# Output projection inside the attention loop, one-hot pairs and bias additions among the key-value products, and the second normalisation by groups of row tiles

## The reference, cut to what matters

```python
xn = layernorm(x)
x = x + gnn(xn) + mix(xn)          # first normalisation
x = x + ffn(layernorm(x))          # second normalisation

# mix: linear attention, 8 heads of 64
q, k, v = split(xn @ w_qkv)
q, k = elu(q) + 1, elu(k) + 1
kv = k.T @ v                        # for each head
z = 1 / (q @ sum(k) + 1e-6)
mix = concat((q @ kv) * z) @ w_out + b_out

# gnn: four experts of two mean-aggregating layers, two chosen for each row
gates = softmax(xn @ gate_W + gate_b); top2(gates)
# ffn: a shared expert and the best 3 of 16 experts, each silu(gate) * up, then down
```

## Time and profile before

| | us |
|---|---|
| median of three runs (1374.01 to 1377.84) | 1375.5 |
| profiled execution | 1378.77 |
| its span | 1376.5 |
| PE busy | 1276.0 (93%) |
| VectorE busy | 717.5 (52%) |
| ScalarE busy | 426.8 (31%) |
| GpSimd busy | 250.6 (18%) |

### The profile page before, as it was taken

How to read it: one execution, slowest core, us unless ns; L and a number is a source line. 1 busy time by engine, 2 the same in 40 slices (tenths; PEclk the granted TensorE clock), 3 DMA queues, 4 the chain that set the end, 5 groups by cost and what they waited for, 6 DMA issues and landing times.

```text
span 1376.5 us, 20320 instructions
## 1 busy us (share of the span) xinstructions
PE 1276.0 (93%) x6004; PEld 978.7 (71%) x6005; DVE 717.5 (52%) x1906; ACT 426.8 (31%) x760; POOL 250.6 (18%) x297
## 2 busy tenths in 40 slices
PE   5799999989999999999999988598999999999994
PEld 4454452668787887888788877377878888887883
DVE  5797765736454355236423624465454455446552
ACT  2022222335344134224322323321342233225331
POOL 2300000303302202310232013114701111111111
PEclk8599996899999999999999999799999999999998
DMA  9500000063524514441545153116673355237522
GB/s 352 217 1 1 1 31 0 1 196 120 154 70 146 142 58 146 101 137 50 161 104 134 54 160 81 74 16 188 186 227 61 56 143 138 55 54 211 149 50 34
DMA packets 72211, 146.62 MB, mean 107 GB/s; under 512 B 11826, under 2 KB 12560, under 8 KB 72148
## 3 DMA queue, kind: packets, MB, share of 16 engines
q1 hardware_dynamic: 54468, 99.41, 21.4%
q0 software_dynamic: 17680, 46.43, 16.0%
HBM read 87.15 MB, written 58.67 MB: 106 GB/s over the span
## 4 chain that ended last, share of the span: by engine, by line
PE 75%; DMA 7%; DVE 7%; issue 5%; POOL 3%; ACT 1%; DVEq 0%; SPq 0%; POOLq 0%; ACTq 0%
PE B L1869 19%; PE B L1721 15%; PE B L1513 15%; PE B L1728 8%; PE B L1664 7%; PE B L1805 3%; PE B L1556 2%; DMA xg<-slots 2%; PE B L1752 2%; DMA arow<-counts,idxA 2%; POOL chosen_ids L605 1%; POOL slots L720 1%; PE B L1850 1%; DMA out_rows<-y,y_tok 1%; PE B L1911 1%
## 5 line engine op out<-in xcount | busy, mean ns | idle before, releaser
L1869 PE MATMUL B<-GUWH,xtH 128*128 (+1 forms) x344 | 145.1, 422 | 0.8 <-DVE xtL L1346 0.8
L711 POOL DMA_INDIRECT out_rows<-y,y_tok x44 | 68.5, 1558 | 381.5 <-ACT y L944 371.5
L1869 PE MATMUL B<-GUWH,xtL 128*128 (+1 forms) x344 | 136.6, 397 | 0.0
L1869 PE MATMUL B<-GUWL,xtH 128*128 (+1 forms) x344 | 136.5, 397 | 0.0
L1090 DVE TENSOR_SCALAR key<-iota_key,keyT,neg_win 128x320 bf16<-128x320 int16 x240 | 89.7, 374 | 0.0
L1664 PE MATMUL B<-GH,conv 128*128 128x512 f32 x210 | 82.2, 392 | 3.0 <-ACT conv L836 3.0
L1664 PE MATMUL B<-GL,conv 128*128 128x512 f32 x210 | 81.9, 390 | 0.0
L1869 PE MATMUL B<-DNWH,htH 128*128 x176 | 75.3, 428 | 1.7 <-DVE htL L1346 1.7
L1869 PEld LDWEIGHTS B<-GUWH,xtL 128*128 128x128 f32 x344 | 65.0, 189 | 15.8
L830 ACT ACTIVATE hsXH<-XT 128x512 fp32r<-128x512 f32 x40 | 25.3, 631 | 162.9 <-PE B L1721 160.8
L1089 DVE TENSOR_SCALAR low<-iota_low,lowT 128x128 bf16<-128x128 int16 x240 | 62.9, 262 | 22.6 <-PE B L1556 21.4
(11 more groups left out here) (364 smaller groups left out, 2839.2 us busy)
## 6 DMA issues: line engine op xcount, KB each, us to landing
raw<-in_L_ffn_expert_gate_up SPq DMA_DIRECT2D x16, 1024.0 KB, 5.3
slots<-fill SPq DMA_DIRECT2D x5, 2112.0 KB, 19.9
hidden<-tr SPq DMA_DIRECT2D x40, 256.0 KB, 2.0
xg<-slots SPq DMA_DIRECT2D x34, 264.0 KB, 2.7
raw<-in_L_ffn_expert_down SPq DMA_DIRECT2D x8, 1024.0 KB, 5.8
counts<-astage SPq DMA_DIRECT2D x10, 648.0 KB, 3.0
W1R<-in_L_gnn_Wr SPq DMA_DIRECT2D x4, 1024.0 KB, 5.9
W1R<-in_L_gnn_Wl SPq DMA_DIRECT2D x4, 1024.0 KB, 8.3
```

What stands on the lines that cost most here:

```text
L711: pool.indirect_dma_start(out=out, out_offset=bass.IndirectOffsetOnAxis(ap=y_tok[:, 0:1], axis=0), in_=y[:, :], in_offset=None, compute_op ...
L1869: last = pe.matmul(bank, rows[a][:, k, :], weights[b](k), start=k == 0 and n == 0, stop=k == KD - 1 and n == 2)
```

## The change

- **Front.** The gate logits stand behind the query products 1 to 10, a tile each, in bank `B[5]`; the windows' bounds behind query product 0. VectorE's work on the gate is cut in four: `gate_maximum` behind the query features, `gate_softmax`, `gate_choice` and `expert_ranks` between the last residuals.
- **Features.** ScalarE computes Relu of -t and then Exp of minus that (`below`); VectorE's minimum is gone.
- **Window pairs.** Six among the query products, thirteen among the key-value products (three of them between a key and a value product), one behind the denominators, none among the output rows.
- **Bias and low parts.** VectorE adds `bo` a tile at a time in the key-value loop, and forms `XN_L` in the attention loop; ScalarE makes `XN_H` ahead of that loop. GpSimd does neither.
- **Denominators.** The three chunks go to rows 0, 32 and 64 of one bank (`DEN` = 72 rows), with one addition and one reciprocal; the masks `heads` have 72 rows, and GpSimd builds them behind the last key and value products.
- **Output projection.** Rows 0 to 5 stand in the attention loop, behind its steps 5, 6, 7, 9, 10 and 11 (`O_AFTER`), rows 6 to 9 behind it. The counts of the adjacency are ready (`at_ready`) ahead of the last residuals, and the aggregation starts with the sum of its first tile, its `count_rows` coming behind.
- **Second normalisation** (`normalise_groups`): statistics, square root and rows of one group of three tiles at a time; `variance(c+1)` comes ahead of `rows(c)`.
- **Last addition.** `add_chosen` reads the row index ahead of its wait for the epilogue.

```diff
-PAIR_AFTER_Q = {2 * p + 1: p for p in range(6)}
-PAIR_AFTER_KV = {i: 6 + i for i in range(NT)}
-PAIR_AFTER_O = {2 * q + 1: 16 + q for q in range(4)}
+PAIR_AFTER_Q = {2: 0, 4: 1, 6: 2, 8: 3, 10: 4, 11: 5}
+PAIR_AFTER_K = {2: 8, 5: 12, 8: 16}
+PAIR_AFTER_V = {0: 6, 1: 7, 2: 9, 3: 10, 4: 11, 5: 13, 6: 14, 7: 15, 8: 17, 9: 18}
+PAIR_AFTER_DEN = 19
+O_AFTER = {5: 0, 6: 1, 7: 2, 9: 3, 10: 4, 11: 5}
+DEN = 72
...
@@ gpsimd
-        pool.wait_ge(S["small_in"], 16 * 3)
-        pool.wait_ge(S["xn_done"], NT)
-        pool.tensor_tensor(X[:, :, :], X[:, :, :], bo[:, :].unsqueeze(1).to_broadcast([P, NT, D]), ALU.add)\
-            .then_inc(S["bias_added"], 1)
-
-        for i in range(NT):
-            pool.wait_ge(S["xn_h"], i + 1)
-            pool.tensor_tensor(XN_L[:, i, :], XN[:, i, :], XN_H[:, i, :].bitcast(F32), ALU.subtract).then_inc(S["xn_l"], 1)
+        pool.wait_ge(S["k_pe"], NT)
+        pool.wait_ge(S["v_pe"], NT)
+        link(pool.memset(heads[:, :, :, :], 1.0))
+
+        link(pool.affine_select(out=heads[:, :, :, :], in_=heads[:, :, :, :], compare_op=ALU.is_ge, fill=0.0,
+                                base=0, pattern=[[32 * P // 2, 3], [P, HP], [1, P]], channel_multiplier=-P // 2))
...
-            wait_first(pool, "ep_done", g + 1)
+            wait_first(pool, "y2_added", g * 16 + 16)
             take(2, g)
             wait_first(pool, "g_idx", taken)
+            wait_first(pool, "ep_done", g + 1)
...
@@ scalar
+        def below(dest, bank, n, done_sem):
+            act.activation(dest, bank, ACT.Relu, scale=-1.0).then_inc(S["ft_relu"], 1)
+            act.wait_ge(S["ft_relu"], n + 1)
+            act.activation(dest, dest, ACT.Exp, scale=-1.0).then_inc(S[done_sem], 1)
...
-        act.wait_ge(S["kv_pe"], HP)
         act.wait_ge(S["wqkv_in"], 32)
         act.activation(WO[1][:, :, :], WO[0][:, :, :], ACT.Copy).then_inc(S["wo_h"], 1)
+        window_pair(PAIR_AFTER_DEN)
+        act.wait_ge(S["kv_pe"], HP)
+        for n in range(NT):
+            act.activation(XN_H[:, n, :], XN[:, n, :], ACT.Copy).then_inc(S["xn_h"], 1)
         for n in range(12):
...
+        def deviation(c):
+            g = slice(c * X_TILES, min((c + 1) * X_TILES, NT))
+            act.wait_ge(S["var_done"], c + 2)
+            act.activation(rstd[:, 1, g], rstd[:, 0, g], ACT.Sqrt).then_inc(S["std_done"], 1)
+
+        deviation(0)
+        deviation(1)
...
         for i in range(NT):
+            if i in (X_TILES, 2 * X_TILES):
+                deviation(i // X_TILES + 1)
+            if i == 2 * X_TILES:
+                act.preload_act_table(ACT.Sigmoid)
             act.wait_ge(S["xt_pe"], NT + i + 1)
...
@@ vector
             dve.wait_ge(S[exp_sem], n + 1)
-            link(dve.tensor_scalar(e_tile, e_tile, 1.0, None, ALU.min))
             dve.scalar_tensor_tensor(dest, bank, 0.0, e_tile, op0=ALU.max, op1=ALU.add).then_inc(S[done_sem], 1)
...
+        gate_maximum()
         for i in range(NT):
             feature(i, K[:, i, :], expo[i % 2][:, :], B[2 + i % 2][:, :], "k_exp", "k_done")
-            hot_pair(PAIR_AFTER_KV[i] + 1)
+            if i == 0:
+                dve.wait_ge(S["small_in"], 16 * 3)
+            last = dve.tensor_tensor(X[:, i, :], X[:, i, :], bo[:, :], ALU.add)
+            if i == NT - 1:
+                last.then_inc(S["bias_added"], 1)
+            if i in PAIR_AFTER_K:
+                hot_pair(PAIR_AFTER_K[i] + 1)
+            hot_pair(PAIR_AFTER_V[i] + 1)
...
+            variance(0)
+            for c in range(1, len(groups)):
+                variance(c)
+                rows(c - 1)
+            rows(len(groups) - 1)
...
@@ tensor
             if n == 0:
-                pe.wait_ge(S["ex_max"], 1)
+                window_bounds()
+                pe.wait_ge(S["small_in"], 16 * 3)
+            elif n <= NT:
+                gate_logits(n - 1)
...
+        for chunk, (c, w) in enumerate(CHUNKS):
+            for h in range(HP):
+                last = pe.matmul(B[5][0:DEN, 0:w], KS[:, h, chunk * DEN:(chunk + 1) * DEN], QT[:, h, c:c + w],
+                                 start=chunk == 0 and h == 0, stop=chunk == 2 and h == HP - 1, skip_group_check=True)
+        last.then_inc(S["den_pe"], 1)
+        window_pair(PAIR_AFTER_DEN)
...
+            product(B[n % 2][:, 0:w], [(KVB[:, h, :], QT[:, h, c:c + w])])
+            if n == 0:
+                pe.wait_ge(S["mix_setup"], 2)
+                pe.wait_ge(S["den_done"], 1)
+            product(B[2 + n % 2][:, 0:w], [(heads[:, n // HP, h, :], den[:, 0:w])]).then_inc(S["at_pe"], 1)
+            if n in O_AFTER:
+                output_rows(O_AFTER[n])
...
-            count_rows(i)
+            if i == 0:
+                pe.wait_ge(S["conv_done"], 1)
+            else:
+                count_rows(i)
...
+            if i == 0:
+                pe.wait_ge(S["o_done"], NT)
+                count_rows(0)
+            else:
                 transpose_rows_out(i - 1)
```

More of the change, by code:

```diff
@@ L809, in _ @@
         at_high(11)
-        for n in range(NT):
-            act.activation(XN_H[:, n, :], XN[:, n, :], ACT.Copy).then_inc(S["xn_h"], 1)
-        for i in sorted(PAIR_AFTER_O):
-            window_pair(PAIR_AFTER_O[i])
         def w1_high(e, k):
@@ new lines, in windows_done @@
+        def windows_done():
+            dve.wait_ge(S["win_done"], NW)
+            with dve.If(long > 0):
+                more = dve.alloc_register("dve_more")
+                dve.reg_mov(more, 1)
+                with dve.Fori(0, NW) as w:
+                    at = dve.value_load(bounds_i[0:1, bass.ds(w + NW, 1)], min_val=VISITS, max_val=ETP - 1)
+                    end = dve.value_load(bounds_i[0:1, bass.ds(w + 2 * NW, 1)], min_val=VISITS, max_val=ETP - 1)
+                    with dve.If(end > at):
+                        with dve.Fori(at, end) as t:
+                            m = dve.snap(more, min_val=1, max_val=NW * ET)
+                            one_hots(0, 0, bass.ds(t, 1), bass.ds(w, 1)).then_inc(S["lhot_ready"], 1)
+                            dve.wait_ge(S["long_pe"], m)
+                            part = AT[:, :, bass.ds(w * WIN, WIN)]
+                            dve.tensor_tensor(part, part, B[6][:, 0:WC].rearrange("p (a w) -> p a w", a=NT), ALU.add)\
+                                .then_inc(S["long_done"], 1)
+                            dve.wait_ge(S["long_done"], m)
+                            dve.reg_add(more, more, 1)
+            dve.sem_inc(S["at_ready"], 1)
@@ L1134, in _ @@
         for n in range(12):
             (c, w), h = CHUNKS[n // HP], n % HP
-            if n == HP:
-                denominators(2)
             dve.wait_ge(S["at_pe"], n + 1)
@@ L1179, in _ @@
-        dve.sem_inc(S["at_ready"], 1)
+            if n - 1 in O_AFTER:
+                residual(O_AFTER[n - 1])
+            if n >= 2:
+                dve.wait_ge(S["xn_h"], n - 1)
+                dve.tensor_tensor(XN_L[:, n - 2, :], XN[:, n - 2, :], XN_H[:, n - 2, :].bitcast(F32), ALU.subtract)\
+                    .then_inc(S["xn_l"], 1)
+        at_low(11)
+        gating = {6: gate_softmax, 7: gate_choice, 8: expert_ranks}
+        for i in range(O_AFTER[11], NT):
+            residual(i)
+            if i in gating:
+                gating[i]()
@@ L1538, in _, with gate_logits, window_bounds @@
         pe.wait_ge(S["xt_done"], NT)
[L1539 to L1541 removed]
+        def gate_logits(i):
+            product(B[5][:, i * GE:(i + 1) * GE], [(XT[:, k, cols(i)], gw[:, k, :]) for k in range(KD)])\
                 .then_inc(S["lg_pe"], 1)
[L1543 to L1546 removed]
+        def window_bounds():
+            pe.wait_ge(S["edge_bounds"], 1)
+            for k in range(3):
+                last = pe.matmul(B[4][0:1, k * NW:(k + 1) * NW], lohi[:, 2 + k:3 + k], ident[0:NW, 0:NW],
+                                 start=True, stop=True)
+            last.then_inc(S["edge_pe"], 1)
         def window_pair(p):
@@ L1638, in _ @@
                         pe.reg_add(more, more, 1)
-        pe.wait_ge(S["o_done"], NT)
+        for i in range(O_AFTER[11] + 1, NT):
+            output_rows(i)
         def count_rows(i):
@@ L1656, in count_rows @@
                 for a in range(NT):
-                    one(aconv_low, a, False)
+                    last = one(aconv_low, a, False)
+                if i == 0:
+                    last.then_inc(S["ag_low_pe"], 1)
             one(aconv[i % 2], NT - 1, True).then_inc(S["ar_pe"], 1)
```

246 lines of the change are left out of this document (121 added, 125 removed).

## The result

The changed kernel took 1346.5 us (median; 1341.2 to 1347.2), the kernel before 1376.1: a ratio of 0.977, 95% interval 0.975 to 0.979. Run a second time, it took 1344.1 (1342.9 to 1345.2), ratio 0.976 (0.974 to 0.978). The prediction was 1339, range 1322 to 1364, faster with 0.93. The first profiled execution took 1341.2 us, span 1339.5, against 1342 in the sum; before had a span of 1376.5. By the medians of the two series the change gave 29.6 and 33.8 us, by the spans of the two profiles 37.0; the sum had 36.7.

A forecast was written before the change was run, and what follows sets the result against it. PE was taken as the bound in the key-value and attention loops, with waits on VectorE and GpSimd in front. Terms of -21.3, +9.7, +3, -22.6, -5 and -0.5 summed to -36.7: 1342 profiled, 1339 us median, range 1322 to 1364.

The forecast's parts named there:

- Front and query loop: Start to end of query loop: gate logits, bounds and choice leave the path, loop ends at 83.9 instead of 105.2, -21.3 us.
- the 4 us kept for the clock: Query loop: allowance for the granted clock coming up, +2.4 us at the least, twice that with a relapse; +4 taken.
- Rival (d): Query loop: gate logits spread between query products hold the clock at 1.2 GHz, +45 us, 1384; chance 0.04.
- Key-value loop: Key-value loop: three more window pairs on PE, 4.9, and three waits of 1.6 in doubled steps, 4.8; +9.7 us.
- Rival (c): Key-value loop: VectorE takes over and every pair waits, another ten waits of 1.2 us, 1351; chance 0.08.
- Key-value products to denominators: Between these stages: GpSimd builds masks while VectorE makes the twentieth pair of hots; +3 us, ends 0 and +8.
- Attention loop and output rows: Denominators to start of aggregation: 69.6 us instead of 91.8, ScalarE's earlier counts conversion gives back 0.4; -22.6.
- step-2 stall: Attention loop: ScalarE's ten `XN_H` copies precede the first factor, so step 2 starts 17.5 us after the first denominator product.
- The clock term: Attention loop: waits and two-product steps make PE less dense, so the clock falls until the first output rows; +5 us.
- Rival (a): Attention loop: the clock doesn't fall, with 72 rows instead of 8 and output rows between; -5 us, 1334; 0.75 with forecast and (e).
- no gap: Start of aggregation: count rows come behind the first sum, its counts converted before, so the 5.9 us gap goes.
- Second normalisation: Second normalisation: rows by groups of three tiles, written at about 869 instead of 874.97; -5 us, ends -9 and +1.

The follow-up runs named there:

- The masks' run: The changed kernel, with GpSimd building the masks only after VectorE has copied all key-value products, while PE makes the denominators: 1337.7 us (0.972).
- the 72-row run: The kernel before, with only the denominators and their masks laid over 72 rows instead of 8: 1369.1 us (0.995).
- the run with the logits ahead: The changed kernel, with all eighty gate-logit instructions put back ahead of the first query product: 1355.7 us (0.986).
- the run with late memsets: The changed kernel, with GpSimd clearing the expert buffers only after VectorE has written all ten normalised row tiles: 1342.8 us (0.977).

## Why the prediction came out right, step by step

*Front and query loop (-21.3; -22.9).* Right, with both halves shown by runs. The first product starts at 25.27 and the loop ends at 82.31, forecast 83.9. Of the 4 us kept for the clock none was needed in the first profile and 2.0 in the second; in four of the ten profiles with this front it fell once, from about 39 or 40 us. The first window pair took 3.83 us, so 2.0 of waiting in place of 1.5, and PE waits 0.98 for the windows' bounds, which no term had. Rival (d), gate logits that hold 1.2 GHz, is a real effect when they stand in one row (14.42 us); eight between two query products did not hold it: where the clock fell, it was back within 3.5 us.

*Key-value loop (+9.7; +9.4).* The size came out by its own working: 1.52 us of waiting in steps 2, 5 and 8, forecast 1.6, single steps of 8.5. Moving the additions showed that VectorE's queue makes it, though an addition gives back 0.45 and not its full 0.69. No run puts the minimum back on VectorE, so what moving it gave isn't shown. Rival (c) fell: VectorE is busy for 83.03 of 95.19 us and waits in the single steps.

*Key-value products to denominators (+3; +4.5).* The mechanism was named, the size was not: VectorE lost 2.85 us, and PE's wait of 2.73 was followed, in both profiles, by a half clock worth 1.7 that no term had. The masks' run takes both away. The Trainium skill (SBUF — State Buffer, SBUF: two separate sides) says that GpSimd and some VectorE instructions, those in a two-port mode among them, share one pair of SBUF ports as an exclusive lock, held for a whole instruction by whichever starts first. The trace agrees on the hold: a one-hot of 0.24 us took 1.63 and 1.54, ending with the GpSimd instruction beside it, and 1.28 beside the low parts in the 72-row run.

*Attention loop and output rows (-22.6 with the aggregation's start; -24.0).* The step-2 stall was right: step 2 came 17.28 us after the first denominator product, forecast 17.5. Several sizes were off, and that they nearly cancel is luck. The clock term, +5, measured 1.6 in both profiles (in five other runs with the same stall the low clock lasted twice as long), and its reason was wrong: I argued that two-product steps make PE less dense. In the kernel before, the fall came with masks over 8 rows; over 72 rows, same order, it did not come, although PE had pauses there. In the changed kernel the fall came behind the stall, and went with it when the copies were moved. Rival (a), no fall in this loop, didn't come true as it stands; its argument "72 rows instead of 8" is what the 72-row run bears out. Steps cost 1.43 to 1.63 instead of 1.83, which the 72 rows give too, and rows 0, 3 and 6 wait 0.53, 0.40 and 0.76. And "no gap" in front of the aggregation was right, but not its continuation: 1.22 and 0.97 us of waiting and 1.6 of half clock inside it, which the prediction didn't see, because it followed the counts' conversion, but neither the copies between two transpositions that follow each other directly nor the store of the first counts behind the loads on SP's queue.

*Second normalisation (-5; -2.5).* Over-sized. The rows came early, as forecast, but GpSimd's memsets held them (4.60 us for three). The prediction named that and only put it into the end of +1. How much they held hung on the moment at which they began: in six other profiles with this stage unchanged the difference to the kernel before is 3.7 to 4.4 us.

*Median.* I carried over that a profiled execution lies 3.3 us above the median. Here the first one lay 5.3 below and the second 0.8 below. That is most of the miss of 5 to 7.5 us. That the sum, 1342, met the profiled 1341.2 is partly luck: the profiled execution before was the slowest of its series and the first one after the fastest, and the larger misses of the stages, -1.6, +1.5, -1.4 and +2.5, cancel. The spread of single executions belongs in the range, not in the middle.

Two of the signs that were set for being wrong showed, though small: the clock of 0.5 in the query loop of the second profile, and steps of the attention loop in which PE waits for VectorE once output rows are in it (0.53 and 0.40 us).

What stays open: why the expert layers and the normalisation differ by 2 us or so between executions, why 72 rows keep the clock up where 8 don't, and why the clock falls behind some waits of PE and not behind others of the same length.

## What to carry to other kernels

When work moves to another engine, look at what its new neighbour does in those microseconds: GpSimd's memsets, masks and additions held VectorE's one-hots, row writes and a subtraction beside them for up to their full length (10.63 us for 0.20), though not its statistics (three in 1.86 us beside memsets, 1.88 without), and a stall of 2 to 3 us on PE was in most profiles paid a second time by a lower clock behind it. When a stage becomes shorter, follow the transfers that used to land in it, store by store on their queue; the wait that appears next is often theirs. And take the gain apart before giving credit: here most of what the title puts first, output rows inside the loop, came from masks over more rows and from the closed gap.

## What the runs showed that I had not expected

- The granted clock went from 1.00 to 0.50 without PE standing still, in two kinds of work: eighty products of four columns (0.50 from 28.4 us in the run with the logits ahead, 3.1 us into them), and the loop with masks over 8 rows (217.2 in the kernel before). Masks over 72 rows, in the same order, ran at 1.00 for 30.08 us.
- It also went to 0.50 around waits of 2.43 and 2.73 us; without these waits it stayed at 1.00 in the same products. But a wait did not always bring it down: it stayed at 1.00 behind 2.72 us in the run with late memsets and behind 2.62 in the 72-row run, and of ten profiles with the wait of 1.22 in the aggregation it fell in six.
- VectorE's row writes took 4.60, 3.02 or 1.46 us for the same three tiles, depending on where in them GpSimd's memset began.
